# The diagonal score tile of a relative-position attention on two halves of TensorE's columns

## What is computed

```python
q, k, v = (proj(W, b) for ...)                  # (B, 16, 512, 8)
idx = clip(pos[None, :] - pos[:, None], -20, 20) + 20
attn = softmax((q @ k^T + einsum('bhqd,qkd->bhqk', q, rel_k[idx])) / sqrt(8))
x = x + (attn @ v + einsum('bhqk,qkd->bhqd', attn, rel_v[idx])) @ Wo.T + bo
x = x + (silu(n @ Wg.T) * (n @ Wu.T)) @ Wd.T    # n = layernorm(x)
```

## Time and profile before

| | |
|---|---|
| median of 3 runs | 1289.37 us (1286.98 to 1291.26) |
| profiled execution | 1285.89 us, its span 1284.2 us |
| TensorE matmuls | 1211.6 us busy, 94% of the span, 26968 instructions |
| TensorE weight loads | 838.5 us, 65% |
| VectorE | 916.4 us, 71% |
| ScalarE | 735.9 us, 57% |
| GpSimd | 576.4 us, 45% |
| mean granted TensorE clock | 0.977 |

### The profile page before, as it was taken

One profiled execution on the slowest core, in us unless ns is written; L12 is line 12 of the kernel. 1 busy time (PEld: TensorE's weight loads), 2 busy tenths in 40 slices (PEclk: granted clock), 3 DMA queues, 4 the chain that ended last, 5 costly groups with the idle time before them and its releaser, 6 DMA issues. The chain is left out here.

```text
span 1284.2 us, 60118 instructions
## 1 busy us (share of the span) xinstructions
PE 1211.6 (94%) x26968; PEld 838.5 (65%) x26976; DVE 916.4 (71%) x1751; ACT 735.9 (57%) x1382; POOL 576.4 (45%) x1079
## 2 busy tenths in 40 slices
PE   4788589999999999999999999999999999999998
PEld 3555256676667666666766667677666667767675
DVE  5887777777777777777777777777777776156664
ACT  5787156665666666666666666666666666623332
POOL 5986434453544444544434354544444544022221
PEclk9999579999999999999999999999999999999999
DMA  4576200201111110202020211111110200022321
GB/s 142 185 238 217 66 24 20 59 24 54 37 42 46 32 56 27 63 15 68 10 69 28 59 32 55 46 40 54 36 53 26 69 9 9 8 71 83 90 75 50
DMA packets 101000, 76.51 MB, mean 60 GB/s; under 512 B 12744, under 2 KB 96520, under 8 KB 100744
## 3 DMA queue, kind: packets, MB, share of 16 engines
q1 hardware_dynamic: 100744, 72.67, 19.0%
HBM read 44.86 MB, written 26.21 MB: 55 GB/s over the span
## 5 line engine op out<-in xcount | busy, mean ns | idle before, releaser
L1166 DVE TENSOR_REDUCE b_mx<-b_a 128x1 f32<-128x512 f32 x1024 | 657.7, 685 | 201.2 <-PE b_a L845 197.7
L1111 ACT ACTIVATE b_p<-b_s 128x512 f32<-128x512 f32 x1024 | 569.6, 595 | 379.9 <-PE b_s L904 238.8
L801 POOL TENSOR_TENSOR qd<-q,one 48x512 bf16<-48x512 bf16 x256 | 266.2, 1040 | 479.6 <-PE b_s L904 461.6
L960 PE MATMUL b_pv<-b_p,vg 128*32 128x256 f32 x4096 | 277.0, 384 | 0.2 <-ACT b_p L1111 0.2
L904 PE MATMUL b_s<-qd,z 112*128 112x32 bf16 (+1 forms) x6016 | 248.4, 188 | 0.6 <-issue 0.6
L845 PE MATMUL b_a<-k,q 48*128 48x512 bf16 x1024 | 204.6, 395 | 22.0 <-DVE b_mx L1166 13.2
L904 PEld LDWEIGHTS b_s<-qd,z 112*128 112x128 bf16 (+1 forms) x6016 | 204.6, 98 | 10.6 <-issue 0.7
L866 PE MATMUL b_s<-q,k 54*128 54x64 bf16 (+5 forms) x4096 | 187.6, 206 | 2.7 <-DMA q<-b_mt 1.2
L866 PEld LDWEIGHTS b_s<-q,k 54*128 54x128 bf16 (+1 forms) x4096 | 112.5, 95 | 96.9 <-PE b_s L866 29.5
L960 PEld LDWEIGHTS b_pv<-b_p,vg 128*32 128x32 f32 x4096 | 117.9, 109 | 64.8 <-issue 20.6
L845 PEld LDWEIGHTS b_a<-k,q 48*128 48x128 bf16 x1024 | 51.5, 94 | 87.3 <-ACT b_p L1111 25.9
(11 more groups left out here) (144 smaller groups left out, 1224.6 us busy)
## 6 DMA issues: line engine op xcount, KB each, us to landing
x<-in_x SPq DMA_DIRECT2D x24, 256.0 KB, 3.3
scratch_qop<-a_parts SPq DMA_DIRECT2D x16, 384.0 KB, 2.5
scratch_kop<-a_parts SPq DMA_DIRECT2D x16, 384.0 KB, 3.1
k<-scratch_kop SPq DMA_DIRECT2D x32, 192.0 KB
q<-scratch_qop SPq DMA_DIRECT2D x32, 192.0 KB
scratch_v<-a_vr SPq DMA_DIRECT2D x16, 256.0 KB, 3.2
k<-scratch_kop SPq DMA_DIRECT2D x32, 128.0 KB
q<-scratch_qop SPq DMA_DIRECT2D x32, 128.0 KB
```

The costliest lines, as they stand in the source:

```text
L801: nc.gpsimd.tensor_tensor(dst, src, one, ALU.mult).then_inc(s["qd_ready"], 1)
L960: nc.tensor.matmul(PV[V32 * a:V32 * (a + 1), g * PT:(g + 1) * PT], v[:, side, half, t, 2 * a + g, :], PR[pos][:, 4 * a + 2 * half + g, :], ...
L1111: nc.scalar.activation(out, src, ACT.Exp, scale=SCALE).then_inc(s["p_ready"], 1)
L1166: nc.vector.tensor_reduce(MX[unit.v % 2][:, h:h + 1], PA[(HP * n + hp) % NBANK][:, :], AX_X, ALU.max, negate=True).then_inc(s["a_used"], 1)
```

## The change

The diagonal tile's products are made on 64 keys at a time, the lower half of the partitions (keys 0 to 63) or the upper one. The 128 queries are four quarters; the first chunk of the tile takes quarters 0 and 3, the second 1 and 2. Score products: two for each one before. Relative products: quarter 0 needs them only on the lower keys, quarter 3 only on the upper ones, 16 each; quarter 1 has 16 on the lower and 10 on the upper keys, quarter 2 has 16 on each. For quarter 3's lower keys, all of which lie far before the query, two products with a new constant matrix `less` (-1 in the three rows from `DROW`, for both heads) and 256 moving columns turn one fixed end into the other. In each chunk both banks are now opened and given their scores first, and the relative products follow, alternating between the two halves of the columns; `s_ready` is raised for the first bank near the end of the chunk and for the second at its end. The matrix `less` is made by four small VectorE operations in the first stage, after batch 12. ScalarE writes each bank's exponentials to the place of its quarter.

```diff
--- before.py
+++ after.py
@@ -271,6 +271,7 @@
     out = k["stored"]
 
     z, slot = m.sb("a_z", [P, ZLO_W + ZHI_W]), m.sb("a_slot", [P, PARTS])
+    ends_ = m.sb("a_ends", [P, HP])
     zp, rkj = m.sb("a_zp", [P, ZLO_W + ZHI_W], BF16), m.sb("a_rkj", [P, 2])
     bvb, rvb = m.sb("a_bvb", [P, P]), m.sb("a_rvb", [P, 2, HD])
     wgi, wui, wdi = m.sb("a_wgi", [P, F], I32), m.sb("a_wui", [P, F], I32), m.sb("a_wdi", [P, FC, P], I32)
@@ -548,6 +549,13 @@
                     for half in range(2):
                         chain(nc.vector.tensor_reduce(k["red"][:, :, half, V16 * half:V16 * half + HD],
                                                       k["ident"][:, :].rearrange("p (b j d) -> p b d j", b=WR, d=HD), AX_X, ALU.add))
+                if n == 12:
+                    for half in range(HP):
+                        at_ = HALF * half + DROW
+                        chain(nc.vector.tensor_reduce(ends_[:, half:half + 1], k["ident"][:, at_:at_ + 3], AX_X, ALU.add))
+                    chain(nc.vector.tensor_scalar(ends_[:, :], ends_[:, :], -1.0, None, ALU.mult))
+                    chain(nc.vector.tensor_tensor(k["less"][:, :], ends_[:, 0:1].to_broadcast([P, HALF]),
+                                                  ends_[:, 1:2].to_broadcast([P, HALF]), ALU.add))
                 if n == 11:
                     dve.wait_ge(s["zeroed"], 2)
                     for p in range(2):
@@ -602,6 +610,8 @@
 CHUNK = ([(0, 0, g) for g in range(NG)] + [(0, 1, g) for g in range(NG)] + [(0, 2, g) for g in range(NG)]
          + [(1, 0, g) for g in range(NG)] + [(1, 1, g) for g in range(NG)] + [(1, 2, g) for g in range(NG)]
          + [(None, 3, n) for n in range(CHUNKS - 6 * NG)])
+QUARTER = P // 4
+QUARTERS = ((0, 3), (1, 2))
 SLICE_DONE = [2 * (max(c for c in range(CHUNKS) if CHUNK[c][1] == pos) + 1) for pos in range(T)]
 BESIDE = [c for c in range(CHUNKS) if CHUNK[c][0] is not None and CHUNK[c][1] in ((1,), (0, 2))[CHUNK[c][0]]]
 
@@ -677,11 +687,9 @@
         first = n + FIRST + min(n, extra)
         return [r for r in range(first, first + (2 if n < extra else 1)) if r < HH * U]
 
-    def blocks(t, i, g):
-
-        half = P // QB // 2
-        near = {0: range(half * g, half * (g + 1)), -1: range(REL // QB), 1: range((P - REL) // QB, P // QB)}
-        return near[t - i]
+    def blocks(t, i):
+
+        return {-1: range(REL // QB), 1: range((P - REL) // QB, P // QB)}[t - i]
 
     def freed(n):
 
@@ -891,16 +899,14 @@
                 return [(bank(pair, c, hp)[:, (hh - hhs[0]) * PT:(hh - hhs[0] + 1) * PT], K[unit.p][r, hh, t * P:(t + 1) * P],
                          Q[unit.p][r, hh, hp, q0:q0 + PT], hh == hhs[0]) for hh in hhs]
 
-            def relative_scores(pair, c, unit, only=None):
+            def relative_scores(pair, c, unit):
 
                 t, g, i = tile_at(pair, CHUNK[c][1]), CHUNK[c][2], unit.i
-                heads, nq = (range(H), 32) if t == i else (range(HG * g, HG * g + HG), 64)
-                for b in blocks(t, i, g):
-                    if only not in (None, QB * b // nq % 2):
-                        continue
+                heads, nq = range(HG * g, HG * g + HG), 64
+                for b in blocks(t, i):
                     x0 = (ZLO_0 if t < i else ZLO_W + ZHI_0) + (t - i) * P - QB * b
                     o_ = bank(pair, c, QB * b // nq % 2)[:, :].rearrange("p (h q) -> p h q", q=nq)[:, :, QB * b % nq:QB * b % nq + QB]
-                    keys = slice(0, P) if t == i else slice(P - STRIP, P) if t < i else slice(0, STRIP)
+                    keys = slice(P - STRIP, P) if t < i else slice(0, STRIP)
                     ins = nc.tensor.matmul(o_[keys], k["z"][0:QROWS, x0 + keys.start:x0 + keys.stop],
                                            QD[unit.v % 2][0:QROWS, heads[0]:heads[-1] + 1, b * QB:(b + 1) * QB],
                                            start=False, stop=True, skip_group_check=True)
@@ -908,10 +914,54 @@
 
             def diagonal_scores(pair, c, unit, n):
 
-                q0, r = unit.i * P + 64 * CHUNK[c][2] + 32 * n, slice(0, HALF + ROWS)
+                q0, r = unit.i * P + QUARTER * QUARTERS[CHUNK[c][2]][n], slice(0, HALF + ROWS)
                 for hh in range(HH):
-                    nc.tensor.matmul(bank(pair, c, n)[:, hh * 64:(hh + 1) * 64], K[unit.p][r, hh, unit.i * P:(unit.i + 1) * P],
-                                     Q[unit.p][r, hh, :, q0:q0 + 32], start=hh == 0, stop=True, skip_group_check=True)
+                    for half in range(2):
+                        keys = slice(HALF * half, HALF * (half + 1))
+                        nc.tensor.matmul(bank(pair, c, n)[keys, hh * 64:(hh + 1) * 64],
+                                         K[unit.p][r, hh, unit.i * P + keys.start:unit.i * P + keys.stop],
+                                         Q[unit.p][r, hh, :, q0:q0 + QUARTER], start=hh == 0, stop=True, skip_group_check=True)
+
+            def diagonal_relative(pair, c, unit, n, half, j):
+
+                quarter = QUARTERS[CHUNK[c][2]][n]
+                b = quarter * QUARTER // QB + j
+                x0, keys = ZLO_W + ZHI_0 - QB * b, slice(HALF * half, HALF * (half + 1))
+                o_ = bank(pair, c, n)[:, :].rearrange("p (h q) -> p h q", q=QUARTER)[:, :, QB * j:QB * j + QB]
+                return nc.tensor.matmul(o_[keys], k["z"][0:QROWS, x0 + keys.start:x0 + keys.stop],
+                                        QD[unit.v % 2][0:QROWS, :, b * QB:(b + 1) * QB],
+                                        start=False, stop=True, skip_group_check=True)
+
+            def diagonal_below(pair, c, unit, n, half):
+
+                q0, r = unit.i * P + QUARTER * QUARTERS[CHUNK[c][2]][n], slice(0, HALF + ROWS)
+                keys = slice(HALF * half, HALF * (half + 1))
+                o_ = bank(pair, c, n)[:, :].rearrange("p (hh hp q) -> p hh hp q", hp=HP, q=QUARTER)
+                for hp in range(HP):
+                    ins = nc.tensor.matmul(o_[keys, :, hp, :], k["less"][r, :], Q[unit.p][r, :, hp, q0:q0 + QUARTER],
+                                           start=False, stop=True, skip_group_check=True)
+                return ins
+
+            def diagonal_band(pair, c, unit):
+
+                every, late = range(QUARTER // QB), range((QUARTER - REL) // QB, QUARTER // QB)
+                if CHUNK[c][2] == 0:
+                    for j in every:
+                        diagonal_relative(pair, c, unit, 1, 1, j)
+                        ins = diagonal_relative(pair, c, unit, 0, 0, j)
+                    ins.then_inc(s["s_ready"], 1)
+                    diagonal_below(pair, c, unit, 1, 0).then_inc(s["s_ready"], 1)
+                    return
+                for j in every:
+                    diagonal_relative(pair, c, unit, 0, 0, j)
+                    diagonal_relative(pair, c, unit, 1, 1, j)
+                for n, j in enumerate(every):
+                    last = diagonal_relative(pair, c, unit, 1, 0, j)
+                    if n < len(late):
+                        ins = diagonal_relative(pair, c, unit, 0, 1, late[n])
+                    if n == len(late) - 1:
+                        ins.then_inc(s["s_ready"], 1)
+                last.then_inc(s["s_ready"], 1)
 
             def scores(pair, c):
 
@@ -931,7 +981,7 @@
                         if n == 0:
                             row_pairs_ahead(pair, c)
                         diagonal_scores(pair, c, unit, n)
-                        relative_scores(pair, c, unit, n).then_inc(s["s_ready"], 1)
+                    diagonal_band(pair, c, unit)
                     return
                 wait_bank(pair, c, 1)
                 if c not in BESIDE:
@@ -1101,7 +1151,8 @@
                         out = PR[pos][:, 4 * g + n:4 * g + 4:HP, :]
                     elif pos == e:
                         src = src.rearrange("p (h q) -> p h q", h=H)
-                        out = PR[pos][:, :, q0 + 64 * g + 32 * n:q0 + 64 * g + 32 * n + 32]
+                        q0 += QUARTER * QUARTERS[g][n]
+                        out = PR[pos][:, :, q0:q0 + QUARTER]
                     elif c in BESIDE:
                         src = src.rearrange("p (h q) -> p h q", h=HG)
                         out = PR[pos][:, HG * g:HG * (g + 1), q0 + 64 * n:q0 + 64 * (n + 1)]
@@ -1442,7 +1493,7 @@
              "x1": [m.sb(f"x1{p}", [P, T, E]) for p in range(2)], "xnT": [m.sb(f"xnT{p}", [P, S]) for p in range(2)],
              "aT": m.sb("aT", [P, S]), "out": {n: m.sem("c_s_" + n) for n in OUT_SIGNALS},
              "eps": m.sb("eps", [P, 1]), "root": m.sb("root", [P, 1]), "neg": m.sb("neg", [P, 1]), "one": m.sb("one", [P, 1]),
-             "minus": m.sb("minus", [P, P], BF16),
+             "minus": m.sb("minus", [P, P], BF16), "less": m.sb("less", [P, HALF], BF16),
              "stored": [m.sem(f"stored{p}") for p in range(2)], "xo_out": [m.sem(f"xo_out{p}") for p in range(2)],
              "kq_in": [m.sem(f"kq_in{p}") for p in range(2)], "v_in": [m.sem(f"v_in{p}") for p in range(2)],
```

## The result

The changed kernel takes 1340.36 us in the median of 4 runs (1336.43 to 1347.43), the kernel before 1290.19 (1286.98 to 1291.26, 4 runs): a ratio of 1.0415, 95% interval 1.0378 to 1.0451. Slower by 50 us, where 1297 was forecast and 1338 was the upper end. The span of the profiled execution is 1337.5 us.

What follows compares the result with a forecast made beforehand. TensorE's full instruction stream was taken as the bound: -6.4 us for products, +13.6 for the new wait, +0.3 for small things, +7.5 in all, on 1289.37 gives 1297 us; likeliest case 1274 to 1317, wider range 1266 to 1338.

Steps and rivals of the forecast that it cites:

- What bounds the kernel: Attention stage: TensorE is full and waits for nobody, so instructions removed shorten the span and additions or new waits lengthen it.
- The products: Diagonal tile: 96 products become 156, in 80 paired steps plus two wide ones; 2.84 us against 2.94, -6.4 us over 64 tiles.
- P: Time of one step of two half-column products in the diagonal chunks: taken as 33 ns; one nanosecond is 5.1 us.
- The Trainium skill's rule: Stationary loads: columns divided by 1.2 GHz, so 64 columns take 53 ns; +112 us, 1401, sharing rival C's chance of 0.11.
- strips at 26 ns: 32-column strip loads: the rule needs 27 ns each, yet they follow at 26; taken as evidence against the rule.
- A load's own record: Changed profile: each 64-column load in the diagonal chunks should last 104 to 107 ns.
- The new wait: After a unit's second diagonal chunk, e = 0: TensorE waits for the first bank's exponential, 0.42 us 32 times, 13.6 us in all.
- First chunk into second: Between a tile's two diagonal chunks: the exponential is covered by a few hundredths, counted as nothing; 3 us if not.
- rival D: Diagonal chunks: halves do not overlap, or issue cannot hold 16 ns for a hundred products; +124 + 14, 1427 us; chance 0.06.

Runs made afterwards that it cites:

- run 3: The changed kernel with the second diagonal chunk finishing bank 0's 26 relative products first, then bank 1's 32: 1329.11 us, ratio 1.0326.
- run 7: The kernel before with some value products moved two chunks earlier, as a control for the same move in the changed kernel: 1417.97 us, ratio 1.1005.
- run 1: The kernel before with each relative product of the diagonal tile issued twice, at the old pace: 1414.08 us, ratio 1.0966.
- run 5: The kernel before with two overwritten streams added: 2048 score products on 64 keys, halves in turn, and 1024 on 128 keys: 1376.07 us, ratio 1.0673.
- run 9: The changed kernel with only the first diagonal chunk new, its scores again 16 products on whole columns: 1287.12 us, ratio 0.9977 to the kernel before.
- run 12: The changed kernel with bank 0 first in the second chunk and both chunks' score products on whole columns: 1307.53 us, ratio 1.0149.

## Why the prediction was wrong

- **What bounds the kernel** held: TensorE's stream goes into the span whole.
- **The products** held. The forecast had -6.4 us; measured 0.11 x 64 = -7.0. P is 31 to 33 ns for the 33 taken. The Trainium skill's rule in "TensorE: Matmul & The Clock Gate", section "LDWEIGHTS (loading the stationary operand)", made it 53 ns, an estimate; the trace doesn't agree, and one half alone is served in 23 to 28 ns. The prediction's ground for doubting that rule was wrong all the same: strips at 26 ns, where the rule gives 27, speak for it, not against it. A load's own record of 113 ns, where I said 104 to 107, says little about its pace.
- **The new wait** held: 13.6 us forecast, 0.34 x 32 = 10.9 in the rows and 11 by run 3. It stands where it was placed, and the output transposes cover it for e = 1.
- **First chunk into second**, counted as nothing: the exponential is covered to within 0.03 us (from L921 to L931 the second chunk takes 610.45 - 609.89 = 0.56 us, the first 0.53). But in the e = 1 tile above, L853 starts 0.44 us after L941 and not 0.32 as in the e = 0 tile, and 21 of the e = 1 tiles are like it. The last exponential had by then been done for 0.8 us; what ended 0.14 us before L853 was VectorE's row maximum, for which the row pair waits. This small wait was in no term: at most 0.12 x 32 = 3.8 us.
- **Sum of these**: -7.0 + 10.9 + 3.8 = +7.7 us at most; the forecast was +7.5, partly by luck, since the exponential's wait came out smaller than forecast and the row pair's, not foreseen, filled the difference. Where nothing starves, a pair takes 30.06 us, and 29.80 before: 0.26 x 32 = 8.3 us.
- **The step that failed** is one sentence of the change's cost: "issue keeps up for at least 32 products at 13 ns; a run of 96 at about 16 ns is not shown". It was seen as open, then priced at nothing in the sum and given 0.06 within rival D, with the overlap of the halves, as if issue were too slow product by product. Issue does hold 16 ns, in every undisturbed chunk. What fails is supply, over stretches longer than a block, and the earlier trace rows, 32 products between slow neighbours, couldn't show it. The missing term is 47 - 8 = 39 us. The profile shows 28.9, 29.6 and 30.1 us of issue waits (42 to 47 pieces) from 130 to 1150 us, against 3.7, 2.8 and 3.7 (9 or 10) before, so 26 us more; with 0.2 hidden in each of 36 more pieces, some 33. The last 6 us fit the clock: past the first 50 us of the stage it is at half for 16 us in the mean of the three profiles and for 1 before, and at the 1.5 us in 3.4 of run 7 that costs 6 to 7 us, an estimate. That the holes bring the clock down is read off: it falls right after one in the rows shown, and there are more such stretches in the kernels with many holes; no run tried it alone.

A hint was in the profile of before: 213 instruction packets for 53944 TensorE instructions, 1284 us by 213 = 6 us each in the mean, and already 3.7 us of waits for issue. Asking how fast a packet can follow another was the check that was left out.

That supply is the cause is shown by runs 1, 5, 9 and 12: the same number of fetches without the density costs nothing, the density alone makes the holes with nothing else running, and taking instructions out of the dense chunks takes about half of the waits out (10.9 to 5.1 us, 18.7 to 10.8). That the packets' distance comes from when the next one is asked for, and not from how fast its 16 KB move, is suggested by the cycle in run 5, but wasn't tried.

## What to carry to other kernels

Count instructions as a resource of their own: if a product is split into two that overlap, the arithmetic gets denser but the stream has to arrive as well, here, in the one long stream that starved, 256 TensorE instructions (128 products with their loads) in 3.66 us in the mean, 29 ns a product. Holes can cost twice, once as time and once more as clock, so look at the granted clock outside the window you chose, and before you compare two runs that both wait. A pace seen in a short group is no evidence for a long one; look at how many instructions stand in a row and at the issue waits, and split only the part where the halves really skip work. Move work into a gap only with a control beside it: the place that it leaves may have needed it as cover.

## What was unexpected of the hardware

- Instructions come in packets of 16 KB on a DMA queue of their own, and a starved TensorE resumes in steps of 256 instructions, every 3.46 to 4.00 us, with no other transfer running.
- At the start of the stream it got through 270 products, 540 instructions, in 6.54 us before the first hole, most of them at a granted clock of 0.50 and some 21 ns a product. One packet came in that time (from 154.67 to 156.30 us), so only about one block was at hand at the start.
- Products on alternating halves of the columns follow each other at 16 ns; on one half alone at 23 (64 moving columns) or 28 ns (32 moving columns), so the fewer moving columns are not the faster ones.
- Short waits of TensorE can cost clock as well as time: in run 7, with waits of 0.7 us all through the attention stage, the granted clock fell to 0.50 in 26 short stretches, at some 1.5 us in each 3.4.
